# One edge tile in every 64 groups comes row by row through ScalarE's queue

## The reference, cut to what matters

```python
n   = _layernorm(x)                                  # (6250, 256)
hx  = jnp.einsum('ni,rio->rno', n, weight)           # 8 relations
agg = jax.ops.segment_sum(hx[edge_type, src], dst, num_segments=6250)
x   = x + agg * 0.5**0.5 + h_bias + (n @ loop_weight) * 0.5**0.5
y   = x + ffn(top half of _layernorm(x) by its router weight) + _layernorm(x)
```

## Time and profile before

| | |
|---|---|
| median of 3 runs | 2165.69 us (2165.49 to 2167.96) |
| the profiled execution, its own time | 2165.49 us |
| its span, first to last instruction | 2163.8 us |
| PE / PEld busy | 1731.9 / 1468.2 us |
| POOL busy | 1574.3 us |
| DVE / ACT busy | 775.9 / 692.3 us |
| gathers on POOL | 1614, from 45.3 to 2077.8 us |
| mean granted TensorE clock | 0.946 |

### The profile page before, as it was taken

How to read it: one execution, slowest core, us unless ns; L and a number is a source line. 1 busy time by engine, 2 the same in 40 slices (tenths; PEclk the granted TensorE clock), 3 DMA queues, 4 the chain that set the end, 5 groups by cost and what they waited for, 6 DMA issues and landing times.

```text
span 2163.8 us, 24160 instructions
## 1 busy us (share of the span) xinstructions
PE 1731.9 (80%) x8696; PEld 1468.2 (68%) x8696; DVE 775.9 (36%) x1720; ACT 692.3 (32%) x1398; POOL 1574.3 (73%) x1765
## 2 busy tenths in 40 slices
PE   1588888778888888888887898887888888888883
PEld 0466677667776766767776677776776677776672
DVE  6433333332333333343243333333323333333336
ACT  3133233333323333333332332333333333233242
POOL 7777777777777777777777777777777777777730
PEclk9899999999999999999999999999999999999995
DMA  9833433433333333333333333433333343343326
GB/s 331 285 105 105 123 106 105 124 105 105 115 114 105 115 114 105 114 115 106 115 115 105 114 115 105 115 115 105 115 115 105 111 118 105 106 124 105 107 84 213
DMA packets 118226, 265.44 MB, mean 123 GB/s; under 512 B 28469, under 2 KB 64036, under 8 KB 118104
## 3 DMA queue, kind: packets, MB, share of 16 engines
q0 software_dynamic: 79024, 219.70, 35.0%
q1 hardware_dynamic: 39080, 44.17, 6.3%
HBM read 244.52 MB, written 19.25 MB: 122 GB/s over the span
## 4 chain that ended last, share of the span: by engine, by line
POOL 57%; issue 19%; PE 16%; DMA 4%; DVE 3%; ACT 1%; DVEq 0%; POOLq 0%; ACTq 0%
POOL messages L432 56%; PE bank L680 6%; PE bank L712 5%; DMA messages<-normed_table,gather_rows 4%; PE bank L743 3%; DVE acc L1122 1%; DVE hidden L798 1%; PE bank L714 1%; PE bank L733 1%; PE bank L690 1%; DMA messages<-in_x 0%; ACT closed L537 0%; ACT L566 0%; ACT hidden L566 0%; POOL acc L423 0%
## 5 line engine op out<-in xcount | busy, mean ns | idle before, releaser
L432 POOL DMA_INDIRECT messages<-normed_table,gather_rows x1614 | 1541.1, 955 | 492.2 <-issue 482.2
L680 PE MATMUL bank<-messages,onehot 128*128 128x256 f32 x3228 | 854.2, 403 | 335.1 <-DMA messages<-normed_table,gather_rows 328.9
L680 PEld LDWEIGHTS bank<-messages,onehot 128*128 128x128 f32 x3228 | 592.2, 197 | 455.5 <-DMA messages<-normed_table,gather_rows 383.7
L973 DVE SCALAR_TENSOR_TENSOR sums<-bank,regular,sums 128x256 f32 x538 | 260.2, 484 | 1288.6 <-PE bank L690 1277.4
L531 ACT ACTIVATE stage<-bank 128x256 f32<-128x256 f32 x538 | 206.6, 384 | 1381.2 <-PE bank L680 1380.7
L712 PE MATMUL bank<-rel_sb,closed 128*128 128x256 f32 x1568 | 354.7, 379 | 2.1 <-ACT closed L537 2.1
L712 PEld LDWEIGHTS bank<-rel_sb,closed 128*128 128x128 f32 x1568 | 297.7, 190 | 43.5 <-ACT closed L537 3.1
L892 DVE TENSOR_TENSOR onehot<-bank,keys 128x768 f32<-128x768 f32 x269 | 254.8, 948 | 0.1
L690 PE MATMUL bank<-ident,stage 128*128 128x128 f32 x1076 | 210.5, 278 | 0.3 <-DVE sums L973 0.3
L743 PE MATMUL bank<-w_sb,hidden 128*128 128x256 f32 x784 | 201.4, 414 | 3.0 <-ACT hidden L566 2.8
L733 PEld LDWEIGHTS bank<-normed_t,w_sb 128*128 128x128 f32 x1568 | 198.6, 205 | 4.5 <-ACT normed_t L558 0.7
(11 more groups left out here) (153 smaller groups left out, 533.0 us busy)
## 6 DMA issues: line engine op xcount, KB each, us to landing
messages<-normed_table,gather_rows POOLq DMA_INDIRECT x1614, 2.8
normed_x<-normed_table SPq DMA_DIRECT2D x12, 512.0 KB, 4.0
acc<-in_x SPq DMA_DIRECT2D x12, 512.0 KB
residual<-resid SPq DMA_DIRECT2D x12, 512.0 KB, 3.5
node_out<-acc SPq DMA_DIRECT2D x12, 512.0 KB
messages<-in_x POOLq DMA_DIRECT2D x6, 896.0 KB, 10.8
normed_table<-messages SPq DMA_DIRECT2D x6, 896.0 KB, 8.5
messages<-residual SPq DMA_DIRECT2D x6, 896.0 KB, 10.5
```

The source lines that it names most:

```text
L432: pool.indirect_dma_start(messages[0:EP, g % RING, j * D:(j + 1) * D], None, table, bass.IndirectOffsetOnAxis(ap=gather_rows[0:EP, g, j:j ...
L680: last = nc.tensor.matmul(banks[g % STAGES][:, 0:D], onehot[0:EP, g % SLOTS, j, :], messages[0:EP, slot, j * D:(j + 1) * D], start=(j == 0 ...
L973: V.scalar_tensor_tensor(sums[:, :, to], banks[TURNS[g % 2]][:, 0:D].rearrange("p (n m) -> p n m", m=W), regular[:, 0:1], sums[:, :, to], ...
```

## The change

In every 64 groups, from group 71 on (71, 135, ..., 519: eight groups, called *sided*), POOL leaves out the third tile. ACT fetches these 128 rows instead, one plain copy of 1 KB a row, two copies in every tick after the copy of the group's sum, into a buffer `side` of two halves. The row numbers come from `src`: SP loads the eight lists of 128 into `side_rows`, and ACT loads four of them into registers in every second tick. The copies of list q are issued in ticks 64q to 64q + 63 and used by PE in group 64q + 71. After tick 511 ACT issues no more of them. Each copy is cut in two pieces of 512 bytes (`GAP` keeps them apart in `side`).

```diff
+    HALF = D // 2
+    GAP = 4
+    EVERY = 64
+    AFTER = 8
+    LOADED = 4
+    def sided(g):
+        return g >= EVERY and (g - AFTER) % EVERY == EVERY - 1
+    def tiles(g):
+        return J - sided(g)
+    def tiles_through(g):
+        return sum(tiles(n) for n in range(g % RING, g + 1, RING))
+    SIDED = sum(sided(g) for g in range(NG))
...
+        side_rows = sb("side_rows", [SIDED, P], I32)
+        side = sb("side", [P, 2, 2, HALF + GAP])
...
+            for q in range(SIDED):
+                sp.dma_start(side_rows[q:q + 1, :], src[q * side_span + side_from:q * side_span + side_from + P].rearrange("(o e) -> o e", o=1)
+                             ).then_inc(side_rows_in, 16)
...
-                for j in range(J):
+                for j in range(tiles(g)):
                     pool.indirect_dma_start(messages[0:EP, g % RING, j * D:(j + 1) * D], None, table,
...
+            def load_side_rows(g):
+                q, first = g // EVERY, 2 * (g % EVERY)
+                registers = [act.alloc_register(f"row{2 * g + n}") for n in range(LOADED)]
+                act.load(registers, side_rows[q:q + 1, first:first + LOADED])
+                return [act.snap(register, donate=True, min_val=0, max_val=N - 1) for register in registers]
+            def side_row(g, n, row):
+                q, to = g // EVERY, 2 * (g % EVERY) + n
+                act.dma_start(side[to:to + 1, q % 2, :, 0:HALF],
+                              table[bass.ds(row, 1), :].rearrange("o (h d) -> o h d", h=2)).then_inc(side_in[q % 2], 16)
+            act.wait_ge(side_rows_in, 16 * SIDED)
+            act.wait_ge(stored, 16 * NCH)
             for g in range(TICKS):
                 if g < NG:
                     stage_group(g)
+                if g < SIDED * EVERY:
+                    if g % 2 == 0:
+                        rows = load_side_rows(g)
+                    for n in range(2):
+                        side_row(g, n, rows[2 * (g % 2) + n])
                 if g - CLOSE in closing:
...
-                pe.wait_ge(gathered[slot], 16 * J * (g // RING + 1))
+                pe.wait_ge(gathered[slot], 16 * tiles_through(g))
+                if sided(g):
+                    q = (g - AFTER) // EVERY
+                    pe.wait_ge(side_in[q % 2], 16 * P * (q // 2 + 1))
...
+                    rows = messages[0:EP, slot, j * D:(j + 1) * D] if j < tiles(g) else side[:, (g - AFTER) // EVERY % 2, :, 0:HALF]
```

More of the change, by code:

```diff
@@ L248, in gnn_ffn_program @@
         gathered = [sem(f"gathered{i}") for i in range(RING)]
+        side_rows_in = sem("side_rows_in")
+        side_in = [sem(f"side_in{i}") for i in range(2)]
         onehot_ready = sem("onehot_ready")
@@ L306, in _ @@
             sp.dma_start(loop_sb[:, :, :], loop_w.rearrange("(k p) o -> p k o", p=P)).then_inc(loop_in, 16)
+            side_span = EVERY * GE
+            side_from = (AFTER + EVERY) * GE - P
+            for q in range(SIDED):
+                sp.dma_start(side_rows[q:q + 1, :], src[q * side_span + side_from:q * side_span + side_from + P].rearrange("(o e) -> o e", o=1)
+                             ).then_inc(side_rows_in, 16)
             def store(c):
@@ L679, in sum_group @@
                         pe.wait_ge(sum_taken, g - LAG)
-                    last = nc.tensor.matmul(banks[g % STAGES][:, 0:D], onehot[0:EP, g % SLOTS, j, :],
-                                            messages[0:EP, slot, j * D:(j + 1) * D], start=(j == 0), stop=(j == J - 1))
+                    rows = messages[0:EP, slot, j * D:(j + 1) * D] if j < tiles(g) else side[:, (g - AFTER) // EVERY % 2, :, 0:HALF]
+                    last = nc.tensor.matmul(banks[g % STAGES][:, 0:D], onehot[0:EP, g % SLOTS, j, :], rows,
+                                            start=(j == 0), stop=(j == J - 1))
                 last.then_inc(summed, 1)
```

## The result

The changed kernel is slower: 2189.97 us in the median of 4 runs (2188.91 to 2199.43), against 2166.82 (2165.49 to 2168.80) of the kernel before, measured beside it. The ratio is 1.0116 with a 95% interval of 1.0086 to 1.0145. The profiled execution is the longest of the four: 2199.43 us, span 2197.7, mean granted clock 0.923 (before: span 2163.8, clock 0.946).

What follows compares the result with a forecast made beforehand. The prediction took POOL's issuing of gathers, one after another without rest, as the bound. 2165.49 us less 10.0 for eight removed steps, with all added work covered, gave 2155.5 us, range 2152 to 2166.

Steps and rivals of the forecast that it cites:

- The removed steps: On POOL: eight gathers left out, each worth one undisturbed step of 1.25 us, 10.0 us in all.
- SP's lists: On SP, ahead of the table's first store: eight 512-byte loads take 2.2 us of 15 idle, so cost nothing.
- the arrival of the buffer: At PE's use of side: last rows issued eight ticks, 30 us, ahead; the wait costs nothing unless ACT runs over 20 us late.
- the queue time, c: On ACT: one tick's row copies, arithmetic and register load cost 1.32 us (lower end 1.06, upper 2.52).
- rival 1: ACT becomes PE's bound, at the deviation, gelu and catching up; from c = 1.76 slower, 2200 us at 1.90; chance 0.16.
- the prediction's own formula: PE's loss to ACT is 7c - 5.75 us a block; what exceeds 6.6 counts 46.5 times over the run.
- the point: Where PE's idle time is used up and ACT becomes its bound: c = 1.76 us a tick.
- the cover: PE's idle time, 6.6 us a block, hides the loss of 3.5 us a block expected from ACT's lateness.
- The gelu: Before PE's product at 613.12: two ticks' copies stand ahead of the gelu, so PE loses 2c - 1.23.
- the deviation's 1.8: At the deviation's table load, leading to normed and PE's transpose with nothing to spare: PE loses c, forecast at 1.32 us.
- The catch-up groups: Where PE catches up on groups already in the ring: some four a block, each losing c - 1.13.
- The end: Behind POOL's last gather: 86.9 us to the span's end, unchanged, so the end moves by the full 10.0 us.

Runs made afterwards that it cites:

- b: The changed kernel without ACT's loads and row copies; PE multiplies a buffer of zeros for the left-out tiles: 2155.03 us, ratio 0.9948 to the kernel before.
- c: The changed kernel with the register load and row copies moved to the end of ACT's tick, behind the block's work: 2153.74 us, ratio 0.9938 to the kernel before.
- d: The changed kernel with the same copies and register loads issued from SP's queue instead of ACT's: 2156.60 us, ratio 0.9956 to the kernel before.
- j: The changed kernel at half the dose: one tile in every 128 groups (4 tiles), one row a tick on ACT: 2162.30 us, ratio 0.9969 to the kernel before.
- k: The changed kernel with twice the tiles (16), one piece a row, copies from SP's queue: 2147.00 us, ratio 0.9909 to the kernel before.
- m: The changed kernel with twice the tiles (16), one piece a row, copies at the end of ACT's tick: 2144.35 us, ratio 0.9896 to the kernel before.
- e: The changed kernel with each row copied as one piece of 1 KB instead of two of 512 bytes: 2154.98 us, one run.
- h: The changed kernel copying fixed rows 0 to 127, with no register load and no arithmetic: 2153.95 us, ratio 0.9944 to the kernel before.
- f: The changed kernel with each row copied in sixteen pieces of 64 bytes instead of two of 512: 2162.02 us, one run.
- g: The changed kernel with eight row numbers loaded in every fourth tick instead of four in every second: 2156.44 us, ratio 0.9949 to the kernel before.
- a: The changed kernel with POOL gathering all three tiles again, ACT's row copies kept but unread: 2186.65 us, ratio 1.0063 to the kernel before.
- i: The changed kernel with copies from SP's queue and twice the tiles (16), four two-piece rows a tick: 2247.62 us, ratio 1.0363 to the kernel before.

## Why the prediction was wrong

**The removed steps were right.** 8 × 1.25 = 10.0 us came out in b, c and d (10.8 to 13.6 between medians), 6.4 for four tiles in j (5.0 by the count), and 20.0 and 22.7 us for sixteen in k and m. The Trainium skill, "DMA: Bandwidth & Descriptors", section "Issuing engines are not separate DMA queues", calls what several issuing engines save usually small; here it is the whole step, and k's 20.0 us of 2167 measure it. SP's lists and the arrival of the buffer cost nothing, as forecast: the changed kernel shows no wait for `side`.

**The first step that failed is the queue time, c.** A row copy was taken at 0.41 us from start to start, with 0.10 of arithmetic, and a register load at 0.60 in two ticks: c = 1.32. The rows show 0.57 for a copy, 0.16 from one copy's end to the next one's start, 0.48 for a load, and 0.49 more for the copy behind it. A tick's instructions then take ACT's queue 2 × (0.57 + 0.16) + (0.48 + 0.49) / 2 = 1.94 us. That is past the 1.76 from which rival 1 holds: by the prediction's own formula 7 × 1.94 - 5.75 - 6.6 = 1.2 us a block are left uncovered, 57 us in all. At its measured size this term alone would have turned the forecast to slower. The formula is off as well, so the 57 us are no measure of the loss. Some of the queue's time runs while ACT still executes the copy of the sum (the copies at 607.00 begin 0.24 us before that ends). So I measured what a tick adds: from the end of the copy of the sum to the end of the tick's last row copy, the mean over four successive ticks of the median of each. PE's waits on ACT are the rows `hidden`, `normed`, `normed_t` and `closed`:

| kernel, copies behind the sum's copy | added us a tick | PE waits on ACT | PE waits for gathers | both | median us |
|---|---|---|---|---|---|
| before | 0 | 6.9 | 328.9 | 335.8 | 2166.82 |
| j, half the rows | 0.57 | 21.0 | 307.2 | 328.2 | 2162.30 |
| e, one piece | 0.71 | 25.0 | 299.4 | 324.4 | 2154.98 |
| h, fixed rows | 0.75 | 25.9 | 299.2 | 325.1 | 2153.95 |
| f, sixteen pieces | 1.15 | 56.3 | 255.0 | 311.3 | 2162.02 |
| g, eight a load | 1.36 | 132.2 | 180.3 | 312.5 | 2156.44 |
| a, copies only | 1.54 | 294.2 | 16.3 | 310.5 | 2186.65 |
| the change | 1.54 | 298.4 | 18.4 | 316.8 | 2189.97 |

The two kinds of wait make up one sum, some 310 to 336 us: ACT's lateness eats PE's waits for gathers, as the prediction said, and costs little until they are used up. That happens between 1.36 and 1.54 us a tick. The same table explains f: its 1.15 us lie under the point.

**The second step that failed is the cover.** The prediction put the point at c = 1.76; by its own formula 1.54 gives 7 × 1.54 - 5.75 = 5.0 us a block, still hidden in 6.6. Two parts of that comparison were wrong. The first shows in the kernel before, in the line ahead of the product at 613.12:

```profile
611.73 1.56 PE L680 MATMUL bank<-messages,onehot 128*128 128x256 f32 x6 [1.91 <-DMA messages<-normed_table,gather_rows]
```

- *Places and spare time.* The gelu was charged 2c - 1.23, 1.9 us at 1.54; PE's wait there grew by (156.7 - 2.8) / 46.5 = 3.3 us a block. The copies are not the whole of it: in the mean of the first 45 blocks the way from the end of the copy of the sum to the gelu's end grew from 4.09 to 6.45 us, by 2.4. The rest is the spare. Before, the product began 1.5 us behind the gelu's end in the mean (1.23 in the block shown), but on the way PE had waited 2.2 us for gathers (1.91 at 611.73); such a wait vanishes as soon as PE is behind, so the spare was part of the 6.6 us and was counted twice. `normed_t`, which also has a copy ahead of it, was not on the list: 0.9 us a block. With the deviation's 1.8 (forecast c) and 0.3 at `closed`, PE waits 6.3 us a block more for ACT. The catch-up groups, charged 4 × (1.54 - 1.13) = 1.6 us a block, show 0.3: in the whole run PE waits 5.3 us for `stage`, and for DVE's sums, which follow it, 11.4 (before: 1.1).
- *PE's own speed.* The cover was worked out with the matmuls of the earlier trace rows. Where PE waits for ACT it comes back at a lower granted clock into long products; it was busy 35.9 us more in the run, 35.9 / 46.5 = 0.8 us a block. The waits, 6.3 + 0.3, just use up the 6.6; with the slower matmuls 0.8 us a block lie beyond it, an estimated 37 us, where 34.5 lie between the forecast and the median. The share of the clock was read from rows; no run takes it away by itself. In a's seven runs the mean granted clock goes with the time (0.949 in the one of 2164.68 us, 0.924 to 0.927 in the four from 2186.65 us up), but that does not say which of the two leads.

**The end.** The forecast had the last gather at 2066.9 and 86.9 us behind it. The profiled execution shows 2084.4, 17.5 later because the ring was full, and 113.3 us behind it, 26.4 more because PE was groups behind. 17.5 + 26.4 = 43.9 us is what lies between 2155.5 and 2199.4. Rival 1 named this mechanism, and 2200 us at c = 1.90; it had a chance of 0.16. That its time comes so near is partly luck, since its formula has the errors told above.

**Still open.** Why two pieces hold the queue longer than sixteen, and why on ACT the copy behind a register load takes 0.49 us more with two pieces, 0.23 with one and nothing with sixteen. It isn't the address (h). On SP the copy behind a load takes 0.04 us more (d, k).

## What to carry to other kernels

A transfer issued from a computing engine stands in that engine's program order: it belongs behind the work that another engine waits for, not ahead of it, and its price there is the issue time with its register work, not the bytes. When idle time is to hide a cost, count each piece of it once: a gap that a late producer makes is gone as soon as the consumer is late itself, and what follows a wait on PE can run slower, as the second product did here. At the double dose one piece a copy was worth far more than the choice of the queue: on SP 100 us (i against k), while SP and ACT's late place lie 2.7 us apart (k against m).

## What the runs showed of the hardware

- Issuing a 1 KB copy from HBM to one partition held ACT's queue 0.213 us in one piece, 0.569 in two and 0.529 in sixteen; SP's 0.225 in one and 0.567 in two.
- With the row number out of a register it took 0.569 us, with a fixed one 0.544.
- The queue begins a transfer while ACT still executes the instruction before it: the copies at 607.00 us beside an ACTIVATE that runs from 606.86 to 607.24. It can begin ahead of that instruction: copies at 627.50 and 628.23 us, the ACTIVATE before them at 628.38.
- PE's matmuls on `side` in i, behind waits of up to 26.9 us, took 634 ns each, where those of k, which hadn't waited for `side`, took 379.
- A kernel close to the point spreads: a ran from 2164.68 to 2193.36 us, j from 2161.42 to 2163.18.
